# Regrouped projection rows and convolution thirds in the scan's prologue, and a split last routing group, in a fused scan, attention and mixture-of-experts kernel

## The chip, the cores and the metric

The kernel runs on 1 core of one Trainium2 chip. The metric is the device time of one launch in microseconds (us). Engines are named as in the profile: PE is TensorE, DVE is VectorE, ACT is ScalarE, POOL is GpSimd and SP is SyncE, which here does nothing but issue DMAs.

## What is computed

The input x is 4 images of 32 x 32 positions and 384 channels, in float32. Three blocks follow each other, each added to its own input:

```
x = x + conv_scan(groupnorm(x))      # in_proj to 2 x 192 channels, 3x3 depthwise conv, silu,
                                     # 4 scans (rows, columns, and both backwards) with 16 states,
                                     # layernorm, gate by silu(z), out_proj
t = t + attn(layernorm(t))           # attention without softmax, one Gram matrix per image, 12 heads
t = t + moe(layernorm(t))            # top-1 routing, 8 experts, 512 slots each, 384 -> 1536 -> 384
```

For each scan direction k the convolved image gives 24 rows for the step sizes ("dt rows") and 2 x 16 rows B and C:

```
x_dbl = einsum('bkdl,kcd->bkcl', xs, x_proj_w)          # 24 + 16 + 16 rows of 1024
dts   = softplus(einsum('bkrl,kdr->bkdl', dts, dt_projs_w) + dt_projs_b)
h     = h * exp(dt * A) + (dt * u) * B ;  y = h . C
```

Attention has no softmax, so it is a product of small matrices per image: a Gram matrix of the tokens, keys and values from it, and one effective weight by which all tokens of the image are multiplied. Routing takes the largest of 8 logits of each token, its place among the tokens that chose the same expert (a running count), and drops what lies beyond 512.

## The kernel before

**Prologue.** Images are taken in pairs: image 0 and 1 are pair p=0, image 2 and 3 are pair p=1. The two images of a pair lie in the two halves of the 128 partitions, and the 192 channels are three thirds (`J = 3`) of 64. PE makes the input projection (`in_proj`, L1048), ACT pads the result (`pad_x`, L668) and gates z (`gate_z`, L677). The nine taps of the convolution of pair 0 are DVE's (`taps`, L1486, after a first tap by ACT, L696). Of pair 1, DVE makes all nine taps of third 0 (`first_third`, L1498 and L1502), and PE makes seven taps of thirds 1 and 2 as matmuls with diagonal weights (`conv`, L1060), to which DVE adds the last two (`last_taps`, L1517). ACT applies silu (`conv_out`, L702), POOL copies each third into column order (`by_columns`, L552).

Then come 24 steps, 12 for each pair, one for each of 4 directions and 3 thirds (`half_of`; step number m = 12p + i). A step is: PE multiplies the dt rows (`delta_product`, L1088, 4 matmul instructions); ACT evacuates twice (`dt_out`, L729 and L730), takes an exponential (`exp_abs`, L735) and later a logarithm (`log_w`, L749); DVE makes `lost_part` (L1549) and, one step behind, `finish` (L1556, L1559, L1563). The 1 + u that `lost_part` reads is made by ACT in the even steps (`one_more`, L744) and by DVE in the odd (L1546). SP stores two results per step (`store_delta`, L401 and L403), in MADE = 4 buffers.

Before every third step there are new projection rows: `x_proj(p, k)` (L1076, 12 matmul instructions) gives, for one direction, the dt rows in partitions 0 to 47 and the B and C rows in partitions 64 to 127. B and C are then split into three bf16 parts: ACT copies the rows (L713) and the first part (L714), DVE subtracts (`split_rest`, L1530), ACT makes the second part (`split_mid`, L718), DVE subtracts again (`split_lo`, L1534). SP stores the parts (`store_parts`, L392, six DMAs, and L395, one). All PSUM results of the prologue but the dt products go through two PSUM slots in a fixed order, `FILL_ORDER`; `slot_free` (L1027) waits until the content two places back has been read. The order of all of this is written out by hand in the loops of each engine (ACT L788, PE L1113, DVE L1602, SP L429); silu of pair 1 stands at step 9 (`SILU_AT`), between two loads of ACT's table.

**Scans.** DVE (L1628, L1645), POOL (L564, L581), PE (L1131, L1147) and ACT (L837, L844) work through 12 tiles of 32 scans. The change doesn't touch them.

**Attention and routing.** Per image b: `mirror`, `keys` (L1302, L1307), `values` (L1316 and, for the bias, L1318), `mixed` (L1325), `bias_row` (L1331), `weights` (L1345) and `attend` for 8 tiles of 128 tokens (L1356) on PE, with transposes and Gram products of the next image between them (L1279, L1285 to L1287). DVE reads the results (L1771, L1775, L1781, L1788), adds the attended tile to the tokens (L1796), takes statistics (`stats`, L1802 and L1806), normalises (`normalise`, L1815), and makes `logits` (L1827 to L1833), `choose` (L1837 to L1843) and `place` (L1850 to L1873). PE makes the counts (`cumsum`, L1337, L1338) and ACT the router's exponential (L932). Routing of an image is done in one piece, and for the last image it is what follows the last attended tile: idx_ok, then eight indirect DMAs of POOL (`scatter`, L619), one for 128 tokens, then the load of expert 0's slots (L514), then PE transposes them (L1393) and begins the experts (L1404, L1416).

Of the kernel before, what the change touches and what calls it, by code (L numbers as in the profile page):

```python
# [5 lines left out]
ALU = mybir.AluOpType  # L6
# [8 lines left out]
S = HW * HW  # L15
# [24 lines left out]
TAPS, PE_TAPS = 9, 7  # L40
# [9 lines left out]
GRP = 32  # L50
A_LOG_MAX = 84.0
# [56 lines left out]
FAR_THIRD = place(3, 0) + 1  # L108
# [3 lines left out]
def half_of(p, i):  # L112

    k, j = divmod(i, J)
    o, dr = k % 2, k // 2
    return k, j, p * OJ + o * J + j, dr
# [37 lines left out]
def hybrid_block_kernel(nc, a, out):  # L154
    with ExitStack() as ctx:
# [43 lines left out]
        xproj_w = ra.take(K, J, P)  # L199
        rest = ra.take(S)  # L200
        rw = Region(arena, PRO, COLS)
        z_sb, xpad, conv_diag = rw.take(J, S), rw.take(J, PADW, PADW), rw.take(J - 1, PE_TAPS, P)
# [18 lines left out]
        d_diag = Region(arena, COLS - P, COLS).take(P)  # L221

# [16 lines left out]
        bkv, head_mask, rt_w = r5.take(2, C), r5.take(C), r5.take(CT, E)  # L239
        bproj, rank8, tri = r5.take(CL), r5.take(NT, E), r5.take(P)  # L240
        xn5, bq_all, col_sum = r5.take(2, C + 1), r5.take(CT, P), r5.take(E)
        base, first_off = r5.take(E), r5.take(E, TB)
# [9 lines left out]
        tot, run = r5.take(E, TB), r5.take(E, TB)  # L252
        pos, keep = r5.take(NT), r5.take(NT)
# [42 lines left out]
        GRAM_PS = (2, 3)  # L296
        SYM_PS, ROW_PS, XK_PS, VK_PS, M_PS, BROW_PS, CUM_PS, WE_PS = 4, 5, (6, 7, 4), 5, (6, 7, 4), 5, 6, (7, 4, 5)

        def attend_bank(i):
# [15 lines left out]
        xp_ok, hi_ok, mid_ok, split_ok = (sem(n) for n in ("xproj_filled", "split_hi", "split_mid", "split_steps"))  # L315
# [25 lines left out]
        tvar_ok, tstd_ok = sem("token_var"), sem("token_std")  # L341
        shift_ok, rexp_ok, hot_ok, cum_ok, idx_ok = (sem(n) for n in ("logits_shifted", "router_exp", "one_hot", "cumsum_filled", "slots_ready"))
        zero_st, scat, ld_w, ld_xe, ld_b2 = sem("zeros_stored"), sem("scattered"), [sem("ld_set0"), sem("ld_set1")], sem("ld_slots"), sem("ld_b2")
# [9 lines left out]
            (conv_w, "conv_w"), (xproj_w, "xproj_w"),  # L353
        ]
        LD_C = 16 * len(CONSTS)
# [10 lines left out]
        def _(sp):  # L366
# [8 lines left out]
            for dst, name in CONSTS:  # L375
                sp.dma_start(dst, a[name]).then_inc(ld_c, 16)

# [8 lines left out]
            def store_parts(p, k):  # L386
                o, dr, x = k % 2, k // 2, p * K + k

                sp.wait_ge(split_ok, 2 * x + 2)
                for part in range(PART):  # L390
                    for m in range(2):
                        sp.dma_start(bc_dram[p * 2 + o, part * SR:part * SR + SR, dr, m],  # L392
                                     parts[H2 + m * SR:H2 + m * SR + SR, k % 2, part]).then_inc(bc_st[k % 2], 16)
                sp.wait_ge(rows_ok, x + 1)
                sp.dma_start(b_dram[p * 2 + o, dr], rows[H2:H2 + SR, k % 2]).then_inc(rows_st[k % 2], 16)  # L395
# [33 lines left out]
            for p in range(NP):  # L429
                store_parts(p, 0)  # L430
                if p == 0:
                    store_z(1, 2)
                for i in range(HALVES):
                    if i % J == 2 and i // J + 1 < K:
                        store_parts(p, i // J + 1)
                    store_delta(p, i)
                    if p == 0 and i == FIRST_DELTAS_AT:

                        sp.wait_ge(ip_ok, len(IN_ORDER))
                        for dr in range(2):  # L440
                            m = dr * OJ
                            sp.wait_ge(dm_st[m % MADE], (m // MADE + 1) * 32)
                            load_delta(0, dr)
                    if p == 1 and i < 2:

                        sp.wait_ge(bc_st[i], K // 2 * PLACED)
                        load_bc(i)
# [54 lines left out]
            sp.dma_start(w1[0], w1_v[0]).then_inc(ld_w[0], 16)  # L502
# [152 lines left out]
        def _(act):  # L655
# [132 lines left out]
            for p in range(NP):  # L788
                for s in range(HALVES + 1):
                    if s < HALVES:  # L790
                        dt_out(p, s)
                        exp_abs(p, s)
                        if s % 2 == 0:
                            one_more(p, s)
# [1246 lines left out]
```

## Time and profile before

| | us |
|---|---|
| median of three runs | 2261.23 (2260.4 to 2262.72) |
| the profiled execution's own time | 2259.55 |
| its span | 2257.7 |
| busy: PE | 1996.3 (88%) |
| busy: DVE | 1579.7 (70%) |
| busy: POOL | 1299.1 (58%) |
| busy: ACT | 1150.4 (51%) |

The span runs from the first to the last instruction that the profiler saw; 1.85 us of the execution lie around it. A busy share is an average over these stages: the prologue (0 to 257.7 us), the scans (to about 1440), the output projection (to about 1497), attention and routing (to 1738.2) and the experts (to the end).

### The profile page before, as it was taken

The page shows a single profiled execution, that of the slowest core. Times are in us where ns is not written, and L with a number is a line of the kernel's source. Part 1 is how long each engine was busy: PE and PEld are TensorE (multiplying, and loading weights), DVE is VectorE, ACT ScalarE, POOL GpSimd, SP SyncE. Part 2 cuts the span into 40 slices and gives each one's busy share as a digit, 9 for nine tenths or more (in the row PEclk, how much of TensorE's full clock was granted, in tenths as well). Part 3 has the DMA queues.
Part 4 walks back from the last instruction along what each step waited for, and adds up shares of the span by engine and source line. Part 5 has one row for each costly group of instructions (what it writes and reads, how often), then busy time and mean ns, then how long its engine had stood idle before and what let it go on. Part 6 is the DMA issues. An engine that isn't in the chain of part 4 may idle for free.

```text
span 2257.7 us, 20191 instructions
## 1 busy us (share of the span) xinstructions
PE 1996.3 (88%) x5862; PEld 923.9 (41%) x5862; DVE 1579.7 (70%) x1480; ACT 1150.4 (51%) x1249; POOL 1299.1 (58%) x464
## 2 busy tenths in 40 slices
PE   7998588888888888888888888989994999999997
PEld 3433133333333333333333333456652555555554
DVE  6899999999999999999999999753553000000000
ACT  4789676767666676766666776211221121111111
POOL 0110399999999999999999999401333011111110
PEclk9996599999999999999999999999997999999999
DMA  5447622133222233222232220511226133333300
GB/s 187 178 162 265 209 75 75 57 107 83 78 70 65 74 102 88 65 74 74 71 96 70 79 65 19 228 42 56 84 85 237 64 121 124 124 119 125 126 24 7
DMA packets 79346, 228.84 MB, mean 101 GB/s; under 512 B 10895, under 2 KB 37121, under 8 KB 77760
## 3 DMA queue, kind: packets, MB, share of 16 engines
q1 hardware_dynamic: 73152, 211.25, 29.1%
q0 software_dynamic: 6144, 16.98, 2.1%
q8 instruction: 24, 0.39, 0.1%
q14 instruction: 26, 0.21, 0.0%
HBM read 166.10 MB, written 64.03 MB: 102 GB/s over the span
## 4 chain that ended last, share of the span: by engine, by line
PE 44%; DVE 26%; issue 17%; POOL 9%; ACT 3%; DMA 1%; DVEq 0%; ACTq 0%; POOLq 0%; SPq 0%
DVE arena L1645 15%; PE ps L1404 11%; PE ps L1416 11%; PE ps L1147 6%; POOL arena L581 5%; POOL arena L564 4%; PE ps L1356 3%; PE ps L1131 2%; DVE arena L1486 2%; DVE ps L1628 1%; PE ps L1144 1%; PE ps L1307 1%; PE ps L1048 1%; PE ps L1345 1%; DVE arena L1556 1%
## 5 line engine op out<-in xcount | busy, mean ns | idle before, releaser
L581 POOL TENSOR_TENSOR arena<-arena 128x2048 f32<-128x2048 f32 x192 | 871.3, 4551 | 17.6 <-DVE arena L1645 16.6
L1147 PE MATMUL ps<-arena 128*128 128x512 f32 x1536 | 726.5, 595 | 29.0 <-POOL arena L581 28.9
L1645 DVE TENSOR_TENSOR_SCAN arena<-arena,ps 128x1024 f32<-128x1024 f32 x264 | 588.9, 2276 | 0.0
L844 ACT ACTIVATE arena<-ps 128x1024 f32<-128x1024 f32 x384 | 390.7, 1017 | 249.0 <-PE ps L1131 247.1
L1131 PE MATMUL ps<-arena 96*128 (+1 forms) x1296 | 366.6, 384 | 128.1 <-DVE arena L1645 112.9
L1147 PEld LDWEIGHTS ps<-arena 128*128 128x128 f32 x1536 | 287.8, 189 | 288.6 <-issue 192.9
L564 POOL TENSOR_TENSOR arena<-arena 128x1024 f32<-128x1024 f32 x120 | 283.9, 2366 | 94.3 <-DMA arena<-b_rows 94.3
L1943 DVE TENSOR_TENSOR arena<-ps,arena 128x384 f32<-128x384 f32 x32 | 17.8, 558 | 449.7 <-PE ps L1416 449.7
L1628 DVE TENSOR_TENSOR ps<-ps,arena 128x1024 f32<-128x1024 f32 x264 | 310.1, 1223 | 13.2 <-PE ps L1131 13.2
L837 ACT ACTIVATE arena<-arena 128x1024 f32<-128x1024 f32 x264 | 300.7, 1139 | 9.0 <-DVE arena L1645 8.6
L1131 PEld LDWEIGHTS ps<-arena 96*128 96x128 bf16 x1296 | 112.8, 98 | 460.2 <-DVE arena L1645 216.3
L641 POOL DMA_INDIRECT out<-arena x32 | 31.7, 992 | 436.6 <-DVE arena L1948 436.6
L1645 DVE TENSOR_TENSOR_SCAN arena<-ps,arena 128x1024 f32<-128x1024 f32 x120 | 272.8, 2273 | 4.6 <-ACT ps L837 4.2
L1416 PE MATMUL ps<-arena 128*128 128x384 f32 x768 | 250.2, 486 | 0.0
L1404 PE MATMUL ps<-arena 128*128 128x512 f32 x576 | 249.5, 594 | 0.0
L1416 PEld LDWEIGHTS ps<-arena 128*128 128x128 f32 x768 | 145.4, 190 | 101.6 <-issue 3.8
L837 ACT ACTIVATE ps<-arena 128x1024 f32<-128x1024 f32 x120 | 134.1, 1118 | 87.5 <-DVE arena L1645 87.5
L1404 PEld LDWEIGHTS ps<-arena 128*128 128x128 f32 x576 | 109.9, 191 | 136.3 <-issue 134.0
L981 ACT ACTIVATE arena<-ps,arena 128x512 f32<-128x512 f32 x96 | 66.0, 688 | 176.0 <-PE ps L1404 175.9
L614 POOL TENSOR_TENSOR arena<-arena 128x384 f32<-128x384 f32 x32 | 27.0, 874 | 190.7 <-DVE arena L1788 190.7
L988 ACT ACTIVATE arena<-arena 128x384 f32<-128x384 f32 x32 | 16.7, 523 | 232.3 <-DVE arena L1943 232.3
L552 POOL COPY arena<-arena 128x1024 f32<-128x1024 f32 x6 | 14.6, 2454 | 145.7 <-ACT arena L702 145.7
(211 smaller groups left out, 1632.6 us busy)
## 6 DMA issues: line engine op xcount, KB each, us to landing
arena<-b_rows SPq DMA_DIRECT2D x240, 256.0 KB, 4.2
arena<-in_w SPq DMA_DIRECT2D x16, 2304.0 KB, 16.3
delta<-arena SPq DMA_DIRECT2D x24, 512.0 KB, 2.7
delta_x<-arena SPq DMA_DIRECT2D x24, 512.0 KB, 2.7
arena<-delta SPq DMA_DIRECT2D x24, 512.0 KB, 3.6
arena<-delta_x SPq DMA_DIRECT2D x24, 512.0 KB, 4.6
slot_in<-arena SPq DMA_DIRECT2D x8, 772.0 KB, 8.1
arena<-slot_in SPq DMA_DIRECT2D x8, 772.0 KB, 18.0
```

Source lines behind the costliest of these rows:

```text
L564: nc.gpsimd.tensor_tensor(xin[:, x % XRING], xin[:, x % XRING], dux[:, dr], ALU.mult).then_inc(in_ok, 1)
L581: nc.gpsimd.tensor_tensor(hst[:, h:h + 2], hst[:, h:h + 2], c_sb[:, c:c + 2], ALU.mult).then_inc(p2_ok, 2)
L837: nc.scalar.activation(dst, dlt[:, dr], ACT.Exp, scale=a_neg[:, q % OJ, dr, n:n + 1]).then_inc(dec_ok, 1)
L844: nc.scalar.activation(c_sb[:, u % RING], C_PS, ACT.Copy).then_inc(c_free, 1)
L981: nc.scalar.activation(h_sb[:, m], ps[:, 3 + m % 3, :], ACT.Gelu_apprx_tanh, bias=b1_col[:, e, m:m + 1]).then_inc(hg_ok, 1)
L1131: mm = pe.matmul(dst[:, h * 512:(h + 1) * 512], sel_lhs[0:BR, n], bc[0:BR, q % OJ // J, dr, m, h * 512:(h + 1) * 512], start=True, stop=True)
L1147: mm = pe.matmul(Y_PS[:, h * 512:(h + 1) * 512], ident, hst[:, u % HRING, h * 512:(h + 1) * 512], start=False, stop=(u == UN - 1))
L1356: mm = pe.matmul(ps[:, attend_bank(i), 0:CA], xnT[:, b % 2, t, i * P:(i + 1) * P], w_eff[:, t], start=(t == 0), stop=(t == CT - 1))
L1404: mm = pe.matmul(ps[:, 3 + m % 3, :], w1[s][:, t, m * P:(m + 1) * P], xeT[:, s, t], start=(t == 0), stop=(t == CT - 1))
L1416: mm = pe.matmul(ps[:, 6 + i % 2, 0:C], h_sb[:, m, i * P:(i + 1) * P], w2[s][:, m], start=(m == 0), stop=(m == MT - 1))
L1628: nc.vector.tensor_tensor(x, x, dux[:, dr], ALU.mult).then_inc(p1_ok, 1)
L1645: nc.vector.tensor_tensor_scan(h, f, x, 0.0, ALU.mult, ALU.add).then_inc(sc_ok, 1)
```

## The change

It has five parts.

1. `x_proj` is done for two directions at once (the two of one order of positions, forward and backward), but for dt rows ("xd") and B and C rows ("xa") apart: 4 calls per pair as before, 12 matmul instructions each. One direction's rows lie in partitions 0 to 63, the other's in 64 to 127. The 24 steps take the directions in the order 0, 2, 1, 3.
2. The split no longer uses DVE. ACT makes all three parts from PSUM at 128 partitions, and between them PE subtracts the part just made with a bf16 matmul by minus the identity.
3. Of pair 1, DVE makes all nine taps of thirds 0 and 1, before the first step; PE makes all nine taps of third 2, and silu reads PSUM. Silu of pair 1 stands at step 6. ACT makes 1 + u in every third step, DVE in the other two.
4. Attention: the key row is made in all 128 partitions, and the bias of the values is a product on DVE in place of three matmuls with one row.
5. The last image is routed in two halves of four tiles. Its statistics are taken tile by tile, ACT normalises its tiles (Ln and Exp in place of Sqrt), POOL scatters four tiles after each half, and the load of expert 0's slots is issued before that of its second weight, whose wait is now its own.

```diff
-FILL_ORDER.insert(len(IN_ORDER) - 1, ("x", 0, 0))
-FILL_ORDER += [("x", 0, 1), ("conv", 1, 1), ("x", 0, 2), ("x", 0, 3), ("conv", 1, 2)]
-FILL_ORDER += [("x", 1, k) for k in range(K)]
+FILL_ORDER.insert(len(IN_ORDER) - 1, ("xd", 0, 0))
+FILL_ORDER += [("xa", 0, 0), ("xd", 0, 1), ("conv", 1, 2), ("xa", 0, 1)]
+FILL_ORDER += [("xd", 1, 0), ("xa", 1, 0), ("xd", 1, 1), ("xa", 1, 1)]
...
-CONV_AT = {1: (1, 0), 4: (1, 1), 7: (2, 0), 8: (2, 1)}
-LAST_TAPS_AT = {4: 1, 8: 2}
-SILU_AT, NEXT_PAIR_AT = HALVES - 3, HALVES - 2
+CONV_AT = {3: 0, 4: 1}
+SILU_AT = 6
+DT_ROWS_AT = {(0, 2): (0, 1), (0, 8): (1, 0), (1, 1): (1, 1)}
+BC_ROWS_AT = {(0, 0): (0, 0), (0, 5): (0, 1), (0, 10): (1, 0), (1, 3): (1, 1)}
+HI_AT = {(0, 0): (0, 0), (0, 6): (0, 1), (1, 0): (1, 0), (1, 4): (1, 1)}
+K_ORDER = (0, 2, 1, 3)
...
+            for k in range(K):
+                sp.dma_start(xproj_w[:, o, :, :, H2 * dr:H2 * dr + H2],
+                             a["xproj_w"][:, k].rearrange("p j (s c) -> p j s c", s=2)).then_inc(ld_c, 16)
...
+            def split_mid(p, o):
+                act.wait_ge(less_ok, 2 * (p * 2 + o) + 1)
+                nc.scalar.activation(parts[:, o, 1], fill_slot("xa", p, o), ACT.Copy).then_inc(mid_ok, 1)
...
+            def take_part(p, o, part):
+                for h in range(2):
+                    mm = pe.matmul(fill_slot("xa", p, o)[:, h * 512:(h + 1) * 512], minus, parts[:, o, part, h * 512:(h + 1) * 512],
+                                   start=False, stop=True, skip_group_check=True)
...
                     if s + 1 < HALVES:
                         delta_product(p, s + 1)
+                    if (p, s - 2) in HI_AT:
+                        take_mid(*HI_AT[p, s - 2])
                     if p == 0 and s in CONV_AT:
-                        conv(*CONV_AT[s])
+                        conv(CONV_AT[s])
+                    if (p, s - 1) in HI_AT:
+                        take_hi(*HI_AT[p, s - 1])
+                    if (p, s) in BC_ROWS_AT:
+                        x_proj("xa", *BC_ROWS_AT[p, s])
+                    if (p, s) in DT_ROWS_AT:
+                        x_proj("xd", *DT_ROWS_AT[p, s])
...
-            first_third(0, 7)
-            split_rest(0, 0)
-            first_third(7, 8)
-            split_lo(0, 0)
-            first_third(8, TAPS)
+            whole_third(0)
+            whole_third(1)
...
-                    mm = pe.matmul(ps[:, VK_PS, t * P:(t + 1) * P], bkv[0:1, 1, t * P:(t + 1) * P], w_row[0:1, t * P:(t + 1) * P],
-                                   start=False, stop=True, skip_group_check=True)
...
-                nc.vector.tensor_tensor(bd.rearrange("p t c -> p (t c)"), ps[:, VK_PS, 0:C], head_mask, ALU.mult).then_inc(bd_ok, 1)
+                chain.link(nc.vector.tensor_tensor(flat, ps[:, VK_PS, 0:C], w_row, ALU.add))
+                nc.vector.tensor_tensor(flat, flat, head_mask, ALU.mult).then_inc(bd_ok, 1)
...
+            last_token_std(0)
+            last_normalise(0)
             router_exp(B - 1)
+            last_token_std(1)
+            last_normalise(1)
+            router_exp(B)
...
+            b = B - 1
+            attended(b, 0)
+            for i in range(1, 4):
+                attended(b, i)
+                tile_stats(b, i - 1)
+            tile_stats(b, 3)
+            last_means(0)
...
+            last_means(1)
+            place(b)
+            logits(b + 1)
+            choose(b + 1)
+            gates(b + 1)
+            place(b + 1)
```

On PE of the new prologue the order of a step s is then: the dt product of step s+1, the second subtraction, a half of the convolution, the first subtraction, B and C rows, dt rows. On ACT it is: `dt_out`, `exp_abs`, `one_more`, `log_w`, the first part (two copies), the second part, the third part, the dt rows, silu. `b_full`, ACT's copy of the rows in float32, is one buffer; `split_hi` waits until SP has stored the last one.

## Rows read from the trace of the kernel before

**Rows 1.** The stage table, prologue steps: stretch, busy time by engine, PEclk, DMA share, GB/s.
```profile
96.30:146.60 50.30, 48.74 (x107) 19.70 (x106) 42.13 (x38) 47.32 (x47) 0.00 (x0) 0.97 0.47 166
...
173.70:257.70 84.00, 62.45 (x94) 22.18 (x94) 80.62 (x71) 71.13 (x71) 0.00 (x0) 0.62 0.69 247
```

**Rows 2.** Groups by line, 96 to 258 us: busy, mean ns, idle before.
```profile
L1530 DVE TENSOR_TENSOR arena<-ps,arena 64x1024 f32<-64x1024 f32 x7 | 8.6, 1228 | 0.2
L1534 DVE TENSOR_TENSOR arena<-arena 64x1024 bf16<-64x1024 f32 x7 | 8.6, 1223 | 0.2
```

**Rows 3.** VectorE in order of time: start, duration, line, operands, [idle before].
```profile
75.73 5.24 DVE L1486 SCALAR_TENSOR_TENSOR arena<-arena 128x1024 f32<-128x1024 f32 x4
...
81.67 9.51 DVE L1502 SCALAR_TENSOR_TENSOR arena<-arena 128x1024 f32<-128x1024 f32 x6
101.47 1.23 DVE L1549 SCALAR_TENSOR_TENSOR arena<-arena 128x1024 f32<-128x1024 f32 x1 [5.15 <-ACT arena L744]
...
160.94 2.83 DVE L1549 SCALAR_TENSOR_TENSOR arena<-arena 128x1024 f32<-128x1024 f32 x1
...
243.67 1.22 DVE L1549 SCALAR_TENSOR_TENSOR arena<-arena 128x1024 f32<-128x1024 f32 x1
...
248.46 0.69 DVE L1546 TENSOR_SCALAR arena<-arena 128x1024 f32<-128x1024 f32 x1
...
257.75 2.36 DVE L1628 TENSOR_TENSOR ps<-ps,arena 128x1024 f32<-128x1024 f32 x2
```

**Rows 4.** TensorE in order of time.
```profile
96.35 5.42 PE L1076 MATMUL ps<-arena 128*128 128x512 f32 x12
101.70 1.98 PE L1088 MATMUL ps<-arena 48*128 48x512 f32 x4
103.61 6.28 PE L1060 MATMUL ps<-arena 128*128 128x512 f32 x14
...
132.16 6.84 PE L1076 MATMUL ps<-arena 128*128 128x512 f32 x12 [1.56 <-DVE arena L1517]
...
173.73 7.19 PE L1088 MATMUL ps<-arena 48*128 48x512 f32 x8 [7.82 <-ACT arena L713]
```

**Rows 5.** ScalarE in order of time.
```profile
125.00 1.11 ACT L729 ACTIVATE arena<-ps,arena 128x1024 f32<-128x1024 f32 x1
...
127.96 1.05 ACT L749 ACTIVATE arena<-arena 128x1024 f32<-128x1024 f32 x1
...
155.84 1.28 ACT L803 ACT_TABLE_LOAD   x1
...
162.00 1.11 ACT L729 ACTIVATE arena<-ps,arena 128x1024 f32<-128x1024 f32 x1
```

**Rows 6.** DMA queue, 15 to 45 us: share of 16 engines over 30 us.
```profile
q1 hardware_dynamic: 2164, 4.33, 44.2%
arena<-in_xproj_w SPq DMA_DIRECT2D x1, 768.0 KB, 7.8
```

**Rows 7.** Chain of waits, attention: start, us, what.
```profile
1676.18 0.41 PE ps L1318 x2
...
1679.19 0.57 DVE arena L1781
...
1733.50 4.59 DMA arena<-slot_in
```

**Rows 8.** VectorE and GpSimd, end of routing, in order of time.
```profile
1708.41 0.55 DVE L1796 TENSOR_TENSOR arena<-arena,ps 128x384 f32<-128x384 f32 x1
...
1717.46 0.22 DVE L1850 TENSOR_TENSOR arena<-ps,arena 128x64 f32<-128x64 f32 x1
...
1721.08 0.17 DVE L1873 TENSOR_TENSOR arena<-arena 128x8 uint32<-128x8 f32 x1
1722.05 0.97 POOL L619 DMA_INDIRECT slot_in<-arena  x1 [16.77 <-DVE arena L1873]
...
1730.99 0.97 POOL L619 DMA_INDIRECT slot_in<-arena  x1 [0.30 <-issue]
```

More of the change, by code:

```diff
@@ L50 @@
 GRP = 32
+ROUTED = [(b, 0, TB) for b in range(B - 1)] + [(B - 1, 0, TB // 2), (B - 1, TB // 2, TB)]
 A_LOG_MAX = 84.0
@@ L716, in split_mid @@
-            def split_mid(p, k):
-                act.wait_ge(split_ok, 2 * (p * K + k) + 1)
-                nc.scalar.activation(parts[H2:P, k % 2, 1], rest[H2:P], ACT.Copy).then_inc(mid_ok, 1)
+                if p and j == J - 1:
+                    act.wait_ge(cpe_ok, 1)
+                    taps_sum = fill_slot("conv", 1, j)
+                else:
+                    act.wait_ge(conv_ok, p * J + (j + 1))
+                    taps_sum = x if p else tap_sum[:, j % 2]
+                nc.scalar.activation(x, taps_sum, ACT.Silu, bias=conv_b[:, j:j + 1]).then_inc(xc_ok, 1)
@@ new lines, in dt_rows_out, with split_hi @@
+            def dt_rows_out(p, o):
+                x = p * 2 + o
+                act.wait_ge(xd_ok, x + 1)
+                if p:
+                    act.wait_ge(dt_ok, 2 * J * (x - 1))
+                nc.scalar.activation(rows[0:H2 + DR, o], fill_slot("xd", p, o)[0:H2 + DR], ACT.Copy).then_inc(rows_ok, 1)
+            def split_hi(p, o):
+                x = p * 2 + o
+                act.wait_ge(xa_ok, x + 1)
+                if x:
+                    act.wait_ge(rows_st[(x - 1) % 2], ((x - 1) // 2 + 1) * 32)
+                if p:
+                    act.wait_ge(bc_st[o], p * 2 * PLACED)
+                slot = fill_slot("xa", p, o)
+                nc.scalar.activation(b_full[0:H2 + SR], slot[0:H2 + SR], ACT.Copy).then_inc(hi_ok, 1)
+                nc.scalar.activation(parts[:, o, 0], slot, ACT.Copy).then_inc(hi_ok, 1)
@@ L1050, in in_proj, with conv @@
                 mm.then_inc(ip_ok, 1)
-            def conv(j, h):
+            def conv(h):
+                j = J - 1
                 slot = fill_slot("conv", 1, j) if h else slot_free("conv", 1, j)
                 pe.wait_ge(xh_ok, place(3, j) + 1)
-                for tap in range(PE_TAPS):
+                for tap in range(TAPS):
                     dy, dx = divmod(tap, 3)
@@ L1110, in _ @@
                 in_proj(im, j)
[L1111 removed]
+            x_proj("xd", 0, 0)
             in_proj(3, 2)
@@ new lines, in choose, with gates @@
+                nc.vector.tensor_tensor(hot[:, tb], rank8[:, tb], over_e(best[:, tb], n), ALU.is_equal).then_inc(hot_ok, 1)
+            def gates(g):
+                b, lo, hi = ROUTED[g]
+                tb = slice(b * TB + lo, b * TB + hi)
+                dve.wait_ge(rexp_ok, g + 1)
+                chain.link(nc.vector.tensor_reduce(esum[:, tb], logit[:, tb], AX.X, ALU.add))
+                nc.vector.tensor_copy(x2[:, tb, C], token[:, tb])
+                chain.link(nc.vector.reciprocal(gate[:, tb], esum[:, tb]))
@@ L1921, in _ @@
                 logits(b)
-                if ahead:
-                    normalise(b, 1)
-            choose(B - 1)
-            normalise(B - 1, 1)
-            place(B - 1)
+                normalise(b, 1)
+            b = B - 1
[5 more added lines that the diff above has]
+            last_means(0)
+            attended(b, 4)
+            tile_stats(b, 4)
+            logits(b)
+            attended(b, 5)
+            choose(b)
+            attended(b, 6)
+            tile_stats(b, 5)
+            gates(b)
+            attended(b, 7)
+            tile_stats(b, 6)
+            tile_stats(b, 7)
+            last_means(1)
[4 more added lines that the diff above has]
+            place(b + 1)
             def owners(e, s):
```

416 lines of the change are left out of this document (222 added, 194 removed).

## The prediction

> **What bounds the kernel now.** I read the stage table first, for the two stretches of time that the change touches, then each engine in order of time there, then the chain of waits. The scans between them are left as they are, and so are the experts but for the start of the first.
>
> In the steps of the prologue VectorE is the busiest engine: 42.1 of 50.3 us in the first stretch, 80.6 of 84.0 in the last, against ScalarE's 47.3 and 71.1 [rows 1]. So ScalarE leads where VectorE still waits for it, and is close behind it later; neither has much room. TensorE was granted 0.97 of its clock in the first stretch and 0.62 in the last [rows 1]. VectorE starts its steps at 101.47 after 5.15 us of idling and gives way to the scans at 257.75 [rows 3].
>
> At the end of attention the last attended tile is added at 1708.41, the last slot numbers are written at 1721.08, GpSimd's eight scatters start at 1722.05 and the last of them at 1730.99, and then comes the load of the slots, 4.59 us from 1733.50 [rows 7, 8]. All of it is on the chain of waits, and TensorE does nearly nothing in it.
>
> **Prologue, what VectorE is rid of.** Sixteen subtractions of the split go; 14 of them stand in these rows at 1.23 us, 1.25 with the gap: 20.1 us [rows 2]. Four last taps go: a tap is 5.24/4 = 1.31, so 5.2 [rows 3]. Nine taps of third 1 come, the first a one-operand product like L1546 (0.69, 0.72 with the gap): 0.72 + 8 x 1.31 = 11.2 [rows 3]. Four more additions of 1 come: 4 x 0.72 = 2.9. Net 11.2 us less. A step of it is 4.79 (243.67 to 248.46), 5.51 where it adds the 1; 24 steps with 16 such are 24 x 4.79 + 16 x 0.72 = 126.5 [rows 3].
>
> **Where it can start.** The sixth tap of third 0 ends at 91.2 [rows 3]; two more taps (2.6) and third 1 (11.2) end at 105.0. If VectorE never waited it would reach the scans at 105.0 + 126.5 = 231.5, 26 us sooner. It won't be let: ScalarE has 24 x 4.0 us (125.00 to 127.96 + 1.05) [rows 5], eight additions of 1, 19 copies of rows and parts, all taken at 1.05 (a 128-partition instruction of the same length, L749 [rows 5]; they run over the free dimension, so double the partitions is taken as free), and silu of pair 1, which with its table loads took 6.2 (155.84 to 162.00) [rows 5]. That is 96 + 8.4 + 20 + 6 = 130, from about 96.6: 227 if it never waited either. With two engines so equal, what counts is the order in which one is late for the other.
>
> **The steps laid out by hand**, with these prices and for TensorE 5.35 a projection (96.35 to 101.70), 1.9 a dt product (101.70 to 103.61), 6.28/14 = 0.45 a conv instruction, so 8.0 for a half of nine taps (18 instructions), 0.5 to 1 for a subtraction [rows 4]. "starts" is VectorE's first instruction of the step:
>
> - Steps 0 to 3: starts 105, 107, 112, 118. ScalarE, held by the two copies after step 0, gives step 1 at 106.9. TensorE waits 1 us for the second part, makes dt rows to 115, and the dt product of step 4 to 117.
> - Steps 4 to 6: TensorE is the bound. From 117 it has conv (8.0), a product (1.9), conv (8.0), a product (1.9), B and C rows (5.35): to 142. The dt product of step 5 comes at 127 and that of 6 at 137. Starts 123, 130, 141.
> - Step 6 on ScalarE: `log_w` ends at 141.7, the two copies wait for TensorE to 142 and end at 144.1, silu and tables end at 150.0, the dt evacuations and exponential of step 7 at 153.0. Step 7 starts at 153; VectorE has idled 7.5 us before it. GpSimd's three column copies fall into that gap. Before, they fell on VectorE's instructions (L1549 took 2.83 instead of 1.22 [rows 3]).
> - Steps 8 to 23: 17 steps from 7 on are 17 x 4.79 + 12 x 0.72 + 3.65 for the last `finish` = 93.7. ScalarE needs 86 for them, but in clumps. At 13 the two copies come after step 12's three activations: VectorE waits 2 us. At 14 the second subtraction stands behind 12 projection instructions on TensorE (xd rows of pair 1, made in the same step): ScalarE waits 2.5 us for it, and VectorE 3.6 at 15. Three more waits of 0.6 or less, at 10, 18 and 19. Sum 7.
> - The scans start at 153 + 93.7 + 7 = 253.7: **4 us sooner** than 257.75.
>
> TensorE's clock is in these prices only in part. After 1.56 us of idling twelve instructions took 6.84 where they had taken 5.42; after 7.82 us eight products' instructions took 7.19 [rows 4], twice the 1.98 for four. In the layout it idles 1 us before step 3's rows (plus 1.5 us at most) and 5.7 us before step 9, where ScalarE has slack. From both sides: 26 us sooner if nothing waits; later than before if the clock falls in steps 2 to 6 (a rival below).
>
> SP's queue: 14 DMAs (6 us of issuing) now stand before steps 2 and 8 and before 14 and 18's stores, where seven stood at a time. The buffer that each holds up is needed four steps, some 22 us, later; cost nothing. `b_full` is single: the copy of step 16 waits for the store of step 14's, by my layout at 207, when it is due: up to 1 us, hidden by VectorE's own work there.
>
> **Constants.** x_proj's weights come in 256-byte runs, 3072 of them, and dt_w twice. The packets of 15 to 45 us took 44.2% of 16 engines for 30 us, 2164 packets, so 98 ns each [rows 6]; at that price 3072 last 19 us after 21.3, with a few us of landing up to 44. Now they land at 28.6 (20.8 + 7.8). VectorE waits for them at 38.4 and ScalarE at 44.1, and VectorE has 2.2 us of idling behind. So 0, and 2 us at most. The Trainium skill (DMA: Bandwidth & Descriptors, Specifications) puts the smallest transfer at line rate at 512 bytes and has smaller ones read, modified and written; by it the upper end would be the nearer one, and no row here shows such a load.
>
> **Attention.** Each image loses six one-row instructions of TensorE, 0.41 us a pair: 1.23 [rows 7]. For images 0 to 2 the next transposes cover VectorE's longer way (two products in place of one, 0.57 [rows 7] and as much again), and the chain is TensorE's: 3 x 1.23. For image 3 nothing covers it: 1.23 - 0.55. Sum 4.4. Against it, the bias column is made once before the first image, two instructions of about 0.5 on VectorE before a token tile that TensorE waits for: +1.0. If VectorE's way weren't covered, it would be 0.6 less three times; if the 0.41 were hidden, all 4.4.
>
> **Routing.** Laid out the same way from the first attended tile, in the old clock: statistics of four tiles and the means to 1702.8; logits, choice and gates of the first half between the attended tiles (0.55 each [rows 8]); the last one is added at 1709.2 instead of 1708.9; its half's statistics to 1710.9; `place` of the first half, less the gates (0.8 of 3.8, 1717.46 to 1721.25 [rows 8]), 3.1: to 1714.0. Four scatters of 1.28 run from 1714.8 to 1719.9, in time. Logits, choice, gates, counts and `place` of the second half: 1.4 + 1.1 + 0.7 + 0.5 + 3.1 = 6.8: slot numbers at 1720.9, as before. ScalarE's eight normalising instructions a half (0.4 each) end at 1715, before they are asked for. Then four scatters instead of eight: 4 x 1.28 = 5.1, and 0.3 from the numbers: **5.5 us**. The slots' load is 4.59 either way; w2's load stands behind it and has 30 us.
>
> **Sum**: -4.1 - 4.4 + 1.0 - 5.5 = -13.0. The profiled execution took 2259.55 (span 2257.7); 2246.5, and the median of three stands 1.7 above it: **2248**.
>
> **Rivals.**
>
> - *A, TensorE's clock falls in steps 2 to 6*, where it has 34 us of work in series (109.6 to 143.8) that all others wait for. At the price of the idle-led products (7.19 for 8 against 1.98 for 4, 1.8 times) it is 28 us more: 2276. It decides from 13 us more, a stretch at 1.4 times its time. For it: 0.62 in the later stretch, and the waits of 0.3 and 1 us just ahead. Against: once fed, TensorE has no gap from 109.6 on, and in the first stretch, with like gaps, it kept 0.97 [rows 1]. The Trainium skill (TensorE: Matmul & The Clock Gate, Part 1) has the gate open with recent activity; by it the fed stretch stays at 2.4 GHz, as those rows show, and A is the less likely.
> - *B, VectorE hardly waits*, ScalarE's order being kinder than I laid it out: up to 22 us more than my 4, so 2226. For: 126 and 130 us of work in a stretch of 150. Against: the convolution's 16 us on TensorE and silu at step 6 are in series.
> - *C, the attention part is hidden* or eaten by VectorE's extra chain: +4.4, 2252.5. *D, the second half isn't ready sooner* (ScalarE's or VectorE's small instructions cost more beside GpSimd): the scatters' gain goes, 2253.5. *E, the prologue gives nothing*: 2252.
>
> **How the numbers follow.** Forecast 0.62, with an own range of 2242 to 2253. A 0.08, B 0.07, C 0.08, D 0.07, E 0.08. A spreads from 2258 up. The range leaves out B's far end and most of A: 2238 to 2257. What a measurement can't tell from no change is 0.2%, 4.5 us: 2256.7 to 2265.8. Faster: 0.62 + B + C + D + E less a little where two of them meet, 0.88. Same: 0.07, half of A and such meetings. Slower 0.05.
>
> **What would show it.** Right: the first scan product (L1628 of before) near 254; an idle gap of VectorE of 6 to 9 us before step 7; TensorE without a gap over the convolution; VectorE's waits at steps 13 and 15; four scatters after the last slot numbers, and the slots' load 5 to 6 us sooner after the last attended tile; attention 1.2 us shorter per image. Wrong: the steps ending below 245 or after 258, TensorE's conv instructions at 0.8 us, the constants landing after 44, or ScalarE's normalising still running when the second half's scatters could start.

## The result, and the profile after

The changed kernel takes **2248.58 us**, median of four executions (2247.26 to 2250.48), against 2261.47 for the kernel before: 0.9943 [0.9926, 0.9961], 12.9 us less. The profiled execution took 2250.48 (span 2248.7), the longest of its four.

The stage table of after (stretch, busy time of PE, PEld, DVE, ACT and POOL, PEclk, DMA share, GB/s), against [rows 1]:

```profile
50.00:54.00 4.00, 4.00 (x6) 1.70 (x7) 3.89 (x6) 3.88 (x4) 0.00 (x0) 0.57 0.51 131
96.00:104.00 8.00, 8.00 (x16) 3.22 (x15) 7.79 (x7) 5.73 (x6) 0.00 (x0) 0.79 0.26 67
108.00:116.00 8.00, 7.08 (x11) 2.81 (x12) 6.11 (x7) 8.00 (x9) 0.00 (x0) 0.57 0.14 55
116.00:150.00 34.00, 34.00 (x77) 13.51 (x77) 25.01 (x22) 22.95 (x24) 0.00 (x0) 1.00 0.48 174
157.30:258.10 100.80, 73.00 (x126) 25.23 (x126) 92.62 (x84) 85.85 (x88) 0.00 (x0) 0.67 0.70 248
```

The fourth column tells who is the bound: from 116 to 150 TensorE is busy all 34 us at full clock while VectorE is busy 25.0 and ScalarE 22.9 of them; later VectorE is (92.6 of 100.8). Ahead of that the granted clock falls three times, to means of 0.57, 0.79 and 0.57 over the first three stretches.

VectorE of after in order of time, against [rows 3]: the starts of steps 1, 5, 6 and 7, each behind a wait, and the first product of the scans (in brackets the wait, and what ended it):

```profile
109.75 0.69 DVE L1607 TENSOR_SCALAR arena<-arena 128x1024 f32<-128x1024 f32 x1 [3.59 <-ACT arena L777]
...
134.34 0.69 DVE L1607 TENSOR_SCALAR arena<-arena 128x1024 f32<-128x1024 f32 x1 [3.17 <-ACT arena L777]
...
145.36 1.23 DVE L1610 SCALAR_TENSOR_TENSOR arena<-arena 128x1024 f32<-128x1024 f32 x1 [5.41 <-ACT arena L786]
...
157.27 0.69 DVE L1607 TENSOR_SCALAR arena<-arena 128x1024 f32<-128x1024 f32 x1 [7.03 <-ACT arena L777]
...
258.09 2.36 DVE L1675 TENSOR_TENSOR ps<-ps,arena 128x1024 f32<-128x1024 f32 x2
```

The releaser is ScalarE each time, but ScalarE itself waits for TensorE: TensorE of after, against [rows 4]:

```profile
97.69 7.11 PE L1143 MATMUL ps<-arena 128*128 128x512 f32 x12
...
108.92 3.75 PE L1171 MATMUL ps<-arena 48*128 48x512 f32 x4 [1.49 <-ACT arena L772]
...
121.30 7.99 PE L1127 MATMUL ps<-arena 128*128 128x512 f32 x18
129.23 1.98 PE L1171 MATMUL ps<-arena 48*128 48x512 f32 x4
131.14 7.99 PE L1127 MATMUL ps<-arena 128*128 128x512 f32 x18
```

So the prologue ends where it did: 258.09 for 257.75. The end of routing is as forecast. VectorE's last slot numbers, GpSimd's scatters after them, and from the chain of waits the slots' load and the first transposes, against [rows 7, 8]:

```profile
1706.94 0.54 DVE L1858 TENSOR_TENSOR arena<-arena,ps 128x384 f32<-128x384 f32 x1
...
1718.15 0.16 DVE L1963 TENSOR_TENSOR arena<-arena 128x4 uint32<-128x4 f32 x1
```
```profile
1712.68 0.97 POOL L644 DMA_INDIRECT slot_in<-arena  x1 [8.84 <-ACT arena L985]
...
1719.11 0.97 POOL L644 DMA_INDIRECT slot_in<-arena  x1 [1.63 <-DVE arena L1963]
...
1722.94 0.97 POOL L644 DMA_INDIRECT slot_in<-arena  x1 [0.30 <-issue]
```
```profile
1725.52 4.39 DMA arena<-slot_in
1730.04 2.15 PE ps L1482 x9
```

From the last attended tile to the transposes it is 23.1 us; before it was 29.8.

The 12.9 us don't come from where the forecast had them. This table splits the spans of two pairs of profiled executions by the same events (first product of the scans, end of the last scan, first normalised tile of tokens, last attended tile, first transpose of the experts). The second pair is the runs `before_again` and `after_again` below.

| stretch | forecast | first pair | second pair |
|---|---|---|---|
| prologue | -4.1 | +0.3 | -0.1 |
| scans | 0 | -0.2 | 0.0 |
| output projection | 0 | +3.9 | +0.4 |
| attention, with the bias column | -3.4 | -5.5 | -5.5 |
| routing | -5.5 | -6.7 | -6.4 |
| experts | 0 | -0.9 | +0.7 |
| span | -13.0 | -9.1 | -10.9 |

### The profile page after: what moved, and what is told of

Read it like the earlier page. It is cut to its first block, busy times and chain, and to the rows that moved or that the text cites. A ratio compares the mean times of both kernels' runs of the same rounds, so it can differ in the third digit from the quotient of the medians.

```text
span 2248.7 us, 20183 instructions
## 1 busy us (share of the span) xinstructions
PE 1987.4 (88%) x5834; PEld 920.8 (41%) x5838; DVE 1573.0 (70%) x1505; ACT 1145.2 (51%) x1258; POOL 1296.3 (58%) x464
## 4 chain that ended last, share of the span: by engine, by line
PE 47%; DVE 22%; issue 17%; POOL 8%; ACT 4%; DMA 1%; DVEq 0%; SPq 0%; ACTq 0%; POOLq 0%
DVE arena L1692 15%; PE ps L1506 11%; PE ps L1493 11%; PE ps L1233 6%; POOL arena L603 4%; POOL arena L586 4%; PE ps L1443 3%; PE ps L1217 2%; PE ps L1114 2%; DVE ps L1675 2%; PE ps L1230 1%; PE ps L1394 1%; PE ps L1432 1%; PE ps L1143 1%; PE ps L1371 1%
```

## Experiments

**The parts alone, and both kernels once more.** Each part of the diff put into the kernel before by itself.

> The kernel before with the new prologue alone (joint rows, the split by ACT and PE, all nine taps of pair 1's third 0 and 1 on VectorE and of third 2 on TensorE, silu at step 6). Theory, from the trace of the changed kernel: the prologue gives nothing, the first product of the scans at 258 (257.75 before), and the time stands within 2 us of the kernel before's: 2261.5. Rival 1, the prediction's: 4 us less, the scans at 254, 2257.4. Rival 2: the 3.7 us lost at the end of the scans are a consequence of the prologue (another order of arrival there); then it takes 4 us more than before, 2265.

Measured: 2260.54 (kernel before 2261.44), 0.9997 [0.9988, 1.0006]: 0.9 us less, with an interval from 2.7 less to 1.4 more, so the prediction's 4.1 is out. The profiled execution is the fastest of the eleven (2258.67). In it the scans start at 254.65, as rival 1 said, and not at 258. Where they start in the ten others isn't known; that they start later in most, as in two profiles of after, would explain the time, but isn't shown. The theory's time held, its start of the scans did not.

> The kernel before with the attention part alone (key row in all partitions, the bias of the values as a product on VectorE). Theory, from the two traces: the image period is 1.77 us shorter three times, the last image 0.83 and the first 0.3 more, the bias column takes 1.03: 5.4 us less, 2256.1. Rival: the 0.2 us that the other products with the row each lost belong to the routing part, and it is the prediction's 3.4 us, 2258.

Measured: 2256.3, 0.9978 [0.9969, 0.9987], 5.1 us less. The theory held. The rival's 3.4 is out by the trace too: from the first normalised tile to the last attended one it is 216.19 us here, 216.17 and 216.12 in the profiles of after, and 221.66 in both of before.

> The kernel before with the last image routed in two halves and nothing else. Theory, from the two traces: last attended tile to the first transpose of the experts 29.8 to 23.0 us, and 0.8 less in the experts: 7.6 us less, 2253.9. Rival: the experts' 0.8 us is chance of the two executions, then 6.8 less, 2254.7; the prediction's figure was 5.5 less, 2256.

Measured: 2255.64, 0.9974 [0.9963, 0.9984], 5.8 less. In its trace it is 23.07 us from the last attended tile to the transposes (1710.60 to 1733.67), 6.45 and 6.75 less than in the two profiles of before; the experts took 519.4, as before, so their 0.9 was chance, as the rival said. The time's own interval (3.6 to 8.4 less) doesn't tell the rival's 6.8 from the prediction's 5.5; the trace does.

> The changed kernel as it is, for a second profiled execution. Two things are to be told as chance of an execution or property of the kernel. (1) At the end of the scans GpSimd's last read-out and VectorE's three additions start within 0.2 us of each other and one of them is slowed: before, the additions took 3.02 and the read-out 7.16; after, 8.54 and 5.18. Theory: chance, so this profile may show either; where it shows 3.02 and 7.16 the span is some 3 to 4 us shorter. Rival: it is the new kernel's, and it shows 8.5 again. (2) TensorE's granted clock was 0.73 between 96 and 100 us and 0.75 between 48 and 52, in stretches that show 1.00 in the kernel before with the same instructions ahead of them. Theory: chance too, so the start of step 7 (157.27) moves by up to 3 us. Median 2248.6 within 1 us either way.

Measured: 2247.82 (2246.95 to 2252.37), 0.9939 [0.9926, 0.9953]. The profiled one is again the longest, with the same falls of the clock and the same 8.5 us for VectorE's three additions at the end of the scans. My "either way" for both was not settled by it, and needed the kernel before again:

> The kernel before as it is, for a second profiled execution, above all its end of the scans. In the traces of the kernels with one part of the change (two of them have the old prologue's and the old scans' code) the three additions took 8.5 us and the read-out 5.18 beside them, like after; only the trace of before has 3.02 and 7.16. Theory: the forecast's base was a lucky execution, 3 to 4 us too low in this stretch, and the kernel before shows 8.5 as well. Rival: the old kernel keeps 3.02, and the 3.7 us are a cost of the change. Time 2261.4 either way, 2260 to 2263.

Measured: 2261.77, the profiled execution 2263.32. VectorE and GpSimd at the end of the scans, `before_again` first, then (for comparison with an order by which they can't meet) `additions_first` below:

```profile
1414.57 8.55 DVE L1669 TENSOR_TENSOR arena<-arena 128x512 f32<-128x512 f32 x3
```
```profile
1414.79 5.19 POOL L581 TENSOR_TENSOR arena<-arena 128x2048 f32<-128x2048 f32 x1 [0.44 <-DVE arena L1645]
```
```profile
1411.38 2.98 DVE L1718 TENSOR_TENSOR arena<-arena 128x512 f32<-128x512 f32 x3
```
```profile
1414.53 4.51 POOL L605 TENSOR_TENSOR arena<-arena 128x2048 f32<-128x2048 f32 x1 [3.40 <-DVE arena L1718]
```

So 8.5 beside 5.2 is the usual case, in the old kernel as well. Of ten profiles in which the two ran side by side nine show it; the tenth is the one that the forecast started from (3.02 and 7.16). One by one the three additions take 1.03, 5.33 and 2.35 us in `before_again`, and the second ends 0.9 us after the read-out:

```profile
1415.53 5.33 DVE L1669 TENSOR_TENSOR arena<-arena 128x512 f32<-128x512 f32 x1
```

In the trace of before they take 1.06, 1.09 and 1.10, and the read-out, already begun, ends 4.4 us after them. So in either case one engine is held up while the other works; which one, differs. The theory holds: the base of the forecast was the exception, and nothing was lost there by the change. In that execution the whole stretch from the last scan to the first normalised tile took 72.65 us; 76.09 in `before_again`, 76.5 in both of after.

**What bounds the prologue.**

> The changed kernel with only two of the nine taps of third 2 on TensorE (14 of 18 instructions of each half of the convolution left out, so pair 2 and 3's last third is not convolved rightly; all else is done). It takes 12.4 us out of what TensorE has in series between steps 3 and 5. Theory: that series bounds steps 5 to 7 (VectorE's idle 3.2, 5.4 and 7.0 us before them), so VectorE's first two gaps go and step 7 starts 9 to 10 us sooner, at 147 (145 where the clock stays at 1.00 up to 116 us); the time falls by 9 to 10, to 2238. Rival: ScalarE's 130 us of work are the bound and would show as new idling of VectorE at the next steps: step 7 at 153 or later, the time down by 4 or less, 2244.

```diff
-                for tap in range(TAPS):
+                for tap in range(2):
```

It leaves out seven of the nine taps of this third, so what it returns is not the convolution asked for. Measured: 2239.17, 0.99 [0.9885, 0.9915]. VectorE's starts of steps 5, 6 and 7:

```profile
128.35 0.69 DVE L1607 TENSOR_SCALAR arena<-arena 128x1024 f32<-128x1024 f32 x1
...
134.04 1.23 DVE L1610 SCALAR_TENSOR_TENSOR arena<-arena 128x1024 f32<-128x1024 f32 x1
...
145.68 0.69 DVE L1607 TENSOR_SCALAR arena<-arena 128x1024 f32<-128x1024 f32 x1 [6.76 <-ACT arena L777]
```

The waits before steps 5 and 6 are gone, the one for silu stays, step 7 is 11.6 us sooner than in the profile of after (8.6 than in those of its like below). The series on TensorE is the bound, and ScalarE's 130 us are not.

> The changed kernel with the 36 instructions of the convolution in four pieces (5, 4, 5, 4 taps, in steps 3 to 6) instead of two halves, so that a dt product stands behind 4.4 us at most instead of 8, and B and C rows of the second order one step later (step 6; their split at 7). Nothing is left out. Theory: what cost time was dt products standing behind a half, so steps 5 and 6 start at 129.5 and 135 (131.3 and 137.5 where the clock falls) instead of 134.3 and 145.4, step 7 at 145.4 to 148.7 and the scans 6.8 sooner: 2241. Rival: TensorE's total up to silu is the bound and not its order; then silu, which still needs all of it, ends as late, step 7 starts at 155 or later, and the time falls by 2 or less: 2246.

```diff
-CONV_AT = {3: 0, 4: 1}
+CONV_AT = {3: (0, 0, 5), 4: (0, 5, TAPS), 5: (1, 0, 5), 6: (1, 5, TAPS)}   # half, first tap, last tap
-BC_ROWS_AT = {(0, 0): (0, 0), (0, 5): (0, 1), (0, 10): (1, 0), (1, 3): (1, 1)}
-HI_AT = {(0, 0): (0, 0), (0, 6): (0, 1), (1, 0): (1, 0), (1, 4): (1, 1)}
+BC_ROWS_AT = {(0, 0): (0, 0), (0, 6): (0, 1), (0, 10): (1, 0), (1, 3): (1, 1)}
+HI_AT = {(0, 0): (0, 0), (0, 7): (0, 1), (1, 0): (1, 0), (1, 4): (1, 1)}
```

Measured: 2242.88 (2240.86 to 2245.39), 0.992 [0.9906, 0.9933], 4.9 less than `after_again`.

```profile
127.38 0.69 DVE L1607 TENSOR_SCALAR arena<-arena 128x1024 f32<-128x1024 f32 x1 [0.29 <-ACT arena L777]
...
134.10 1.23 DVE L1610 SCALAR_TENSOR_TENSOR arena<-arena 128x1024 f32<-128x1024 f32 x1 [1.11 <-ACT arena L786]
...
145.38 0.69 DVE L1607 TENSOR_SCALAR arena<-arena 128x1024 f32<-128x1024 f32 x1 [4.74 <-ACT arena L777]
...
247.48 2.36 DVE L1675 TENSOR_TENSOR ps<-ps,arena 128x1024 f32<-128x1024 f32 x2
```

With nothing left out step 7 starts as early as with 14 of 18 instructions gone: what cost the time was that the dt products stood behind 8 us of convolution, and ScalarE idled meanwhile. The scans start 7.2 us sooner than in `prologue_only` (6.8 expected).

**TensorE's clock.** The same prologue starts its scans at 258.09, 258.32 and 257.76 in three profiles and at 254.65 and 254.87 in two. The stage table shows where the clock was lower; here `additions_first`, one of the second kind:

```profile
50.00:54.00 4.00, 4.00 (x10) 1.72 (x10) 3.89 (x6) 4.00 (x4) 0.00 (x0) 1.00 0.51 131
96.00:104.00 8.00, 8.00 (x16) 3.02 (x14) 7.79 (x8) 5.05 (x6) 0.00 (x0) 0.83 0.14 41
108.00:116.00 8.00, 7.24 (x16) 3.00 (x14) 7.86 (x8) 8.00 (x10) 0.00 (x0) 0.79 0.32 131
```

All three of the first kind have 0.57 between 50 and 54, both of the second 1.00. The fall at 96 doesn't tell them apart: `additions_first` has it (0.83), `prologue_only` hasn't (1.00).

Of the 3 us, 0.7 to 1.0 come from neither. They are there at 25 us already, in TensorE's very first projection; after, then `additions_first`:

```profile
16.73 8.36 PE L1114 MATMUL ps<-arena 128*128 128x512 f32 x12 [1.20 <-DVE arena L1567]
```
```profile
17.20 6.86 PE L1116 MATMUL ps<-arena 128*128 128x512 f32 x12 [1.20 <-DVE arena L1569]
```

In each the first instructions take 1.06 to 1.19 us and the last 0.59; in after the first seven are slow, in `additions_first` the first four. Where this change comes differs from execution to execution, in the kernel before as well (8.13 us in the profile of before, 7.56 in `routing_only`), and it shifts all that follows. So prologues are better compared from the end of this first projection to the scans:

| | no fall at 50 | a fall at 50 |
|---|---|---|
| old prologue | 232.7 (before), 232.4 (`routing_only`) | 233.2 (`before_again`), 233.2 (`attention_only`) |
| new prologue | 230.3 (`prologue_only`), 230.8 (`additions_first`) | 233.0, 233.1 (both of after), 232.5 (`readout_first`) |

The old prologue loses 0.5 to 0.8 us where the clock falls, the new one 1.7 to 2.8. What the new one saves is 1.6 to 2.4 us without the fall and 0.1 to 0.7 with it.

> The changed kernel with eight more matmul instructions of 512 columns on TensorE whose results nobody reads: two before the group sums of image 2, three before those of image 3 (about 47 to 50 us), three before the dt product of step 3 (about 107 us, where it idles 1.49). They add 1 to 2 us where TensorE is on the path. Theory: the falls of its clock at 50 to 54 and 108 to 114 us follow its idle or nearly idle time just ahead; with it filled the clock stays at 1.00 there, step 7 starts at 154.5 instead of 157.3, and the profiled span and time are 1 to 3 us less than the profiled ones of the changed kernel (2250.5, 2252.4), the median 2247. Rival: the falls come from something else (the moment, or the load of the whole chip); then they stay, and the added instructions cost their 1 to 2 us: 2249 to 2250.

Its stage table, and VectorE's start of step 7:

```profile
50.00:54.00 4.00, 4.00 (x19) 2.40 (x18) 3.45 (x9) 1.70 (x2) 0.00 (x0) 1.00 0.00 0
96.00:104.00 8.00, 8.00 (x19) 3.43 (x19) 7.79 (x8) 7.54 (x7) 0.00 (x0) 1.00 0.26 67
108.00:116.00 8.00, 8.00 (x20) 3.25 (x19) 6.31 (x7) 8.00 (x10) 0.00 (x0) 1.00 0.09 38
```
```profile
155.73 0.69 DVE L1615 TENSOR_SCALAR arena<-arena 128x1024 f32<-128x1024 f32 x1 [7.03 <-ACT arena L777]
```

Measured: 2248.72 (2247.66 to 2249.33), 0.9941 [0.9927, 0.9954]. Up to 150 us no fall is left in this profile. For the one at 108 that tells something: the nine other profiles of the new prologue, with its variants, all have it (0.54 to 0.79 from 108 to 116). The one at 50 is missing in six of these nine with nothing filled in, and the one at 96 in three, so a single profile can't say that the filling removed them. The mean granted clock, 0.970 or 0.971 in all five executions, doesn't say it either: `additions_first` has the same with falls at 96 and 108. Step 7 comes at 155.73, 1.4 later than in an execution without the fall at 50 (0.6 to 0.9 of it from the first projection), and the median is 0.9 above that of `after_again` and 0.1 above the first one. The eight calls are 16 instructions in the trace, of some 0.46 us each: 7.5 us, and not the 1 to 2 expected. So the theory held for the clock in the profiled execution, and the rival for the time; that the added instructions take what the clock gives fits, but isn't shown apart.

**The end of the scans.**

> The changed kernel with GpSimd's very last read-out held until VectorE's three additions of the two orders are done, so that they never run together. Theory: the two slow each other (8.54 and 5.18 side by side against 3.02 for the additions in the profile of before), so the additions take 3.0 us from 1414.2, the read-out 4.5 from 1417.3, and all that follows is as in the profile of before: the output projection 3.7 us sooner, 2244. Rival: the read-out's later end (1421.8 instead of 1419.6) is what the loads and the last sum wait for and takes most of it back: a gain of 1.5 us or less, 2246.5.

```diff
                     pool.wait_ge(c_free, U + 3)
+                    if last and u == UN - 2:
+                        pool.wait_ge(yt0_ok, J)
```

Measured: 2246.88 (2245.46 to 2247.55), 0.9934 [0.992, 0.9947], 0.9 less, which the two intervals don't tell from nothing. The local effect is as expected (the lines above: 2.98 and 4.51; the next step of VectorE 6.0 us after the last scan instead of 10.6). Then it is taken back, in TensorE's instructions of the output projection; `additions_first`, then `after_again`:

```profile
1445.82 1.70 PE L1322 MATMUL ps<-arena 128*128 128x8 f32 x12
1447.37 1.43 PE L1325 MATMUL ps<-arena 128*128 128x8 f32 x6
1448.65 5.36 PE L1289 MATMUL ps<-arena 128*128 128x512 f32 x6
```
```profile
1454.13 0.81 PE L1323 MATMUL ps<-arena 128*128 128x8 f32 x6
1454.80 2.82 PE L1287 MATMUL ps<-arena 128*128 128x512 f32 x6
```

Nearly twice the time for the same instructions, so the lower of the clock's two levels: 3.2 us more in these two rows. The rival's 1.5 or less is what came, by another way than it named. The fall isn't this order's own, though: `fed` (1448 to 1456) and `quarters` (1440 to 1448) have 0.79 in the output projection too, with the additions beside the read-out.

> The changed kernel with the other order: VectorE's three additions wait until GpSimd's last read-out is done, and GpSimd's own additions of the next part until VectorE's are. By the theory of the slowing, the read-out takes 4.5 us from 1414.4 and the additions 3.0 from 1419, end 1422: 0.7 us before the 1422.7 of the profile of after, and the loads go out 0.7 sooner too. Time 2247, 0 to 1 less than the changed kernel. Rival: the first loads, not the additions, set the end; then it is the better of the two orders, since they are issued at 1419 instead of 1421.8: 2244.

Measured: 2250.16 (2247.17 to 2252.09), 0.9946 [0.9933, 0.996], no gain. The read-out took 4.50 from 1414.50, the additions 2.95 from 1419.11, as expected. Three of its five executions, the profiled one too, had the mean clock of 0.968 that goes with the falls in the prologue, so its median says little of this order. By kind there is no gain either: its three at 0.968 took 2250.16 to 2252.09, those of the changed kernel 2249.6 to 2252.37; its two at 0.970 took 2247.17 and 2247.56, those of the changed kernel 2246.95 to 2248.21. The rival's 2244 isn't borne out in any of them.

**Versions that put these together.**

> The changed kernel with the convolution in four pieces and the additions first, as run before, and with the rows of pair 1 later: dt rows of the first order a step later (step 9), B and C rows of the second order two steps later (17), the splits of pair 1 two steps later (14 and 18). Nothing is left out. Theory, from the steps laid out with the durations of the traces: dt rows and splits crowd on TensorE and ScalarE just where they wait for each other at the change of pairs; moved, they cost 5 us less than in the version with four pieces: the scans start at 242.5 (247.5 there), and the time is 2242.9 - 5 - 0.9 = 2237. Rival: TensorE's low clock in those steps (0.50 to 0.85) makes its products the bound wherever the rows stand: the scans at 247, 2241.5.

Measured: 2242.01 (2241.32 to 2245.79), 0.9918 [0.9905, 0.9932]; the scans start at 250.43, 3 us later than in `quarters` and not 5 sooner (0.8 of the 3 were there at the end of the first projection). ScalarE waits for the stores of the deltas and again ahead of the copy of the rows:

```profile
183.90 1.11 ACT L773 ACTIVATE arena<-ps,arena 128x1024 f32<-128x1024 f32 x1 [4.07 <-DMA delta_x<-arena]
214.78 1.02 ACT L753 ACTIVATE arena<-ps 96x1024 f32<-96x1024 f32 x1 [4.37 <-issue]
```

Neither theory nor rival: the steps laid out took SP's queue as free, and with the parts' stores moved later in it the stores of deltas come too late. For the first wait the queue as the cause is read from the releaser, not tested. For the second no releaser is shown; there SyncE's own rows have the two stores of the float32 rows issued from 212.17 to 213.08, behind twelve of the parts from 206.10, and the copy is written to wait for them.

> The changed kernel with the convolution in four pieces and the additions of the two orders held apart from the last read-out, and with the rows of pair 1 where the change has them. Nothing is left out. Theory: the two gains were measured one by one against the changed kernel (2247.8): 4.9 us for the four pieces (2242.9) and 0.9 for the additions (2246.9), the second up to 3.5 where no fall of TensorE's clock takes it back in the output projection. They lie in different stretches and add: 2241, between 2239 and 2242, the scans at 247.5 and the additions 3.0 us long. Rival: the later rows of the kernel run before were what kept it at 2242.0, its scans at 250.4 being chance; then this one has its scans at 250 too and takes 2242.

Measured: **2240.12** (2239.37 to 2243.07), 0.9909 [0.9892, 0.9925]: 21.1 us less than the kernel before beside it (2261.2) and 7.7 less than the changed kernel's 2247.82. It beats both kernels. Its scans start at 249.55, 2 later than in `quarters`, in which the theory was wrong: step 7 stands 2.35 later already (147.73), and the clock was 0.71 from 96 to 100 where `quarters` had 1.00. The other gain is larger than `additions_first` alone showed: from VectorE's additions to the first normalised tile it is 74.90 us here and 77.82 in `quarters`, and the granted clock is 0.79 from 1440 to 1448 in both. With like clocks the order is worth 2.9 us, and 2.8 is what the median fell by.

## Why the prediction was right, and where it wasn't

The forecast was 2248, the time 2248.58. That it came out to 0.6 us is luck: its terms were off in both directions. By the times of the single parts the prologue gave 0.9 us where 4.1 were forecast, attention 5.1 for 3.4 and routing 5.8 for 5.5. That is 11.8 of the 12.9 measured; the last 1.1 is within the intervals.

- **The base** made no error in the forecast, since the sum was taken from the median. But it makes the first pair of profiles mislead: in the profiled execution of before (2259.55) the output projection took 72.65 us instead of 76.1, so this pair shows +3.9 in a stretch that the change leaves alone. The second profiled execution (`before_again`) is 3.8 us longer.
- **What bounds the prologue.** The prediction calls VectorE the busiest engine of its steps. In the first stretch of its own rows TensorE is, with 48.74 of 50.30 us, ahead of ScalarE's 47.32 and VectorE's 42.13. The layout then did make TensorE the bound of steps 4 to 6, rightly.
- **Prologue, -4.1: the step that failed is the price of TensorE in steps 0 to 3.** It took full clock and "1.5 us at most" for a short idle. From the first projection of the steps to the first half of the convolution it laid out 20.65 us (96.35 to 117); it took 22.7 and 22.9 in the two profiles without the fall at 50, and 23.6 in after (97.69 to 121.30). In after the projection took 7.11 instead of 5.35, the dt product after 1.49 us of idling 3.75 instead of 1.9; in `prologue_only` the next projection took 7.75, at a clock of 0.65. The rest is where the steps begin: at 95.6 and 95.5 without the fall at 50, at 97.7 with it, of which no row of the steps tells. Step 7 was laid out at 153.0 and the scans at 253.7; they come at 154.3 and 254.7 to 254.9 in the first kind and at 157.27 and 258.09 in after. Step 7 to the end takes 100.4 to 100.8 us of a forecast 100.7. Part of even the 3 us at 254.7 is the first projection (the table above: 1.6 to 2.4 saved at best). Rival E (2252, the prologue gives nothing) describes the prologue of the profiled execution, and the time of `prologue_only` is near it.
- **The mechanism of it held**: TensorE without a gap over the convolution, 7.99 a half for 8.0, VectorE's wait of 7.03 before step 7 for 7.5, waits at 13 and 15. What I took as given was that the half of 8 us had to stand before a dt product. `quarters` shows 7 us in that order alone.
- **Rival A** (the clock falls in steps 2 to 6, 2276) was partly true: it fell at the head of that stretch, to 0.57 from 108 to 116, and stood at 1.00 once TensorE was fed (116 to 150). The rule of the Trainium skill that stands beside it (TensorE: Matmul & The Clock Gate, Part 1) has the gate open with recent activity; for the fed stretch the trace agrees (1.00). For the fall at 98 it doesn't: in after TensorE had been busy without a gap from 73.3 on, at a clock of 1.00.
- **B** (VectorE hardly waits) is out: 19.2 us of waits up to step 7. **C** (attention hidden) and **D** (the second half of routing not ready sooner) are out by the two single parts, 5.1 and 5.8 us less.
- **Attention, -4.4 + 1.0: mis-sized**, -5.5 in both pairs. The time from image to image fell by 1.77 us (53.53 to 51.76) and not by 1.23, and the column's two instructions took 1.15. I had priced only the rows that went; why the rest of each image got 0.5 us shorter wasn't tried.
- **Routing, -5.5: mis-sized by 1**, -6.4 to -6.7. Four scatters less are 5.1, as taken (1719.11 to 1722.94 in place of 1722.05 to 1730.99). From the last tile to the slot numbers it is 11.2 us, 1.5 less than before where 0.3 was taken; the load gave 0.2.
- **Constants, 0**: VectorE begins its first use of them at 38.54, before at 38.49. The rule of the Trainium skill on pieces under 512 bytes (DMA: Bandwidth & Descriptors, Specifications) made the upper end, 2 us, the nearer one; nothing of it shows in VectorE's start. The four loads of 192 KB took 8.2 us each from issue to landing (median), the one of 768 KB had taken 7.8. The last was issued by 27.9 us, so by the median they had landed at about 36, before VectorE came to them; what the short pieces cost a load that is waited for, no run here shows.

## What to carry to other kernels

Put a long piece of work of an engine that others wait for in slices between the short products they wait for: the order alone was worth 5 to 7 us here, as much as each whole part of the change. Before two profiles are set side by side, take a second one of the old kernel: here the first had one stretch 3.5 us shorter than usual, and a change that doesn't touch it seemed to cost that much. Read the rows of the clock, too, in several executions before a saving is believed or denied: in the prologue they decided over 2 to 3 us, and at the end of the scans they took back 3 of 4.6 us in one profile. And where a forecast hits, test its parts alone: here two of them were off by 1.7 and 3.2 us, in opposite directions.

## What the runs showed of the hardware

- VectorE's additions of 128x512 and GpSimd's read-out of 128x2048, started 0.2 us apart, take 8.5 and 5.2 us side by side and 3.0 and 4.5 apart. Once in ten profiles the split was 3.0 and 7.2. VectorE's second addition took 5.33 us in the usual split and 1.1 in the other. Side by side they save nothing: 8.5 against 7.5 in series, though the third of VectorE's additions (2.35 us) then also runs beside GpSimd's next ones, which take 2.3 in place of 1.5.
- TensorE's clock differs between executions behind the same instructions: twelve projection instructions took 5.42 or 7.11 us with no gap before them (`prologue_only` at 95.64, after at 97.69), and the first twelve of a launch 6.86 to 8.37. With the idles filled, one profile shows 1.00 from 108 to 116, where nine others have 0.54 to 0.79. Why a fall comes at 98 with TensorE busy ahead of it stays open.
